# Expert stage: two up blocks moved ahead of two down blocks, gathers in blocks of three, results in halves

## What is computed

```python
H, E = 4, 24                       # four groups of 1024 tokens, 24 experts
C = math.ceil(2 * S / E)           # 86 places for each expert
def per_group(xf, lw, lb):         # xf: the group's 1024 tokens x 128
    combine, dispatch = top2_dispatch(xf, Wg, C)          # each token goes to two experts
    h = moe_apply(xf, combine, dispatch, W1, b1)          # 128 -> 512, both experts' rows added
    h = relu(layer_norm(h, lw, lb))
    return moe_apply(h, combine, dispatch, W2, b2)        # 512 -> 128
out = layer_norm(out + x, ln_out_w, ln_out_b)
x = x + layernorm(out)
```

## Time and profile before

| | before |
|---|---|
| median of 3 runs | 1206.05 us (1205.61 to 1211.87) |
| profiled execution, its own time | 1214.45 us |
| its span | 1212.7 us |
| PE busy in the span | 910.2 us (75%) |
| ACT busy | 793.9 us (65%) |
| DVE busy | 562.8 us (46%) |
| POOL busy | 378.3 us (31%) |
| mean granted clock of TensorE | 0.88 |

### The profile page before, as it was taken

One profiled execution on the slowest core, in us unless ns is written; L12 is line 12 of the kernel. 1 busy time (PEld: TensorE's weight loads), 2 busy tenths in 40 slices (PEclk: granted clock), 3 DMA queues, 4 the chain that ended last, 5 costly groups with the idle time before them and its releaser, 6 DMA issues. The chain is left out here.

```text
span 1212.7 us, 18733 instructions
## 1 busy us (share of the span) xinstructions
PE 910.2 (75%) x6570; PEld 431.7 (36%) x6570; DVE 562.8 (46%) x1894; ACT 793.9 (65%) x1181; POOL 378.3 (31%) x333
## 2 busy tenths in 40 slices
PE   4746974661599999999999999998499496594740
PEld 4633762330122222222222223323276364463640
DVE  7488767894001444344445153334351225326356
ACT  2133351453699999999999999994476483574720
POOL 6222442543300000000000000115572766866752
PEclk9657996886699999999999999998699698698875
DMA  3000005647921111111112121238786874966821
GB/s 98 1 1 1 1 1 129 162 114 203 324 78 49 52 46 61 52 61 52 61 52 62 53 61 30 64 79 238 163 167 198 136 175 127 169 173 142 154 68 50
DMA packets 83615, 118.37 MB, mean 98 GB/s; under 512 B 8974, under 2 KB 45583, under 8 KB 83410
## 3 DMA queue, kind: packets, MB, share of 16 engines
q1 hardware_dynamic: 67344, 88.72, 24.2%
q0 software_dynamic: 14752, 27.81, 13.6%
q10 hardware_dynamic: 1442, 0.86, 0.3%
HBM read 72.66 MB, written 44.70 MB: 97 GB/s over the span
## 5 line engine op out<-in xcount | busy, mean ns | idle before, releaser
L1466 ACT ACTIVATE s_e<-s_ps 128x1024 f32<-128x1024 f32 x512 | 486.9, 1025 | 30.0 <-PE s_ps L1615 29.4
L1628 PE MATMUL s_acc<-s_e,s_v 128*32 128x512 f32 x2048 | 274.5, 608 | 0.1
L1615 PE MATMUL s_ps<-s_q,s_k 64*128 64x512 bf16 x1024 | 196.0, 389 | 50.2 <-ACT s_e L1466 22.6
L1100 POOL DMA_INDIRECT x_in<-x_tokens,rows_of x72 | 70.2, 976 | 502.2 <-DVE rows_of L1259 456.0
L1615 PEld LDWEIGHTS s_ps<-s_q,s_k 64*128 64x128 bf16 x1024 | 49.2, 93 | 320.7 <-ACT s_e L1466 274.8
L1100 POOL DMA_INDIRECT e_hs<-h_rows,rows_of x72 | 116.3, 1615 | 65.0 <-DMA h_rows<-e_hs 42.0
L1888 PE MATMUL e_pn<-ident,e_hs 128*128 128x128 f32 x288 | 54.1, 307 | 78.4 <-DVE e_hs L2018 57.3
L1904 PE MATMUL e_py<-w,e_ht 128*96 128x128 f32 x768 | 103.0, 282 | 0.0
L1978 ACT ACTIVATE e_ht<-e_pn,ln_hid 128x288 f32<-128x288 f32 x192 | 84.8, 507 | 26.7 <-PE e_pn L1888 26.7
L1904 PEld LDWEIGHTS e_py<-w,e_ht 128*96 128x96 f32 x768 | 92.5, 170 | 0.0
L1962 ACT ACTIVATE l_so<-e_hs 128x512 f32<-128x512 f32 x72 | 45.2, 628 | 65.1 <-DMA e_hs<-h_rows,rows_of 62.4
(11 more groups left out here) (413 smaller groups left out, 1334.9 us busy)
## 6 DMA issues: line engine op xcount, KB each, us to landing
h_rows<-e_hs SPq DMA_DIRECT2D x72, 256.0 KB, 3.1
s_k<-stack_k SPq DMA_DIRECT2D x32, 512.0 KB, 4.5
s_q<-stack_q SPq DMA_DIRECT2D x32, 256.0 KB, 3.2
w<-in_w SPq DMA_DIRECT2D x1, 6144.0 KB, 21.7
y_rows<-e_ys SPq DMA_DIRECT2D x24, 192.0 KB
stack_q<-b_parts SPq DMA_DIRECT2D x8, 384.0 KB, 4.5
stack_k<-b_parts SPq DMA_DIRECT2D x6, 384.0 KB, 4.3
x_res<-in_x SPq DMA_DIRECT2D x4, 512.0 KB, 7.3
```

Source lines behind the costliest of these rows:

```text
L1100: nc.gpsimd.indirect_dma_start(dst, None, rows, bass.IndirectOffsetOnAxis(ap=idx, axis=0), compute_op=op).then_inc(R["landed"][k % FLIGHT] ...
L1466: nc.scalar.activation(E[g % 4][:, 2 * pair:2 * pair + 2, :], pS[pair][:].rearrange("p (a s) -> p a s", a=2), ACT.Exp, scale=SCALE).then_i ...
L1615: last = nc.tensor.matmul(pS[pair][:, a * CH:(a + 1) * CH], K[c % 2][rows, pair, j * P:(j + 1) * P], Q[c % 2][rows, pair, :], start=True, ...
L1628: last = nc.tensor.matmul(acc[hu % 2][32 * h:32 * h + 32, :], V4[c % 2][:, j, h, :], E[g % 4][:, h, :], start=j == 0, stop=j == TB - 1)
```

## The change

The change does five things. PE's fifth step of a group does the last two up blocks first, with the transposes of the last down block among them, and then the last two down blocks; since chunks of two blocks are then alive, there are six buffers of transposed chunks in place of four (`NHT`; the sixth is the tile `l_o`, free by then). The first x_transposes of the next group move from the end of the last up block to the place behind the first h_transposes of a group. POOL's gathers are ordered by blocks of three. The results of a group are gathered, normalised and stored in two halves. And DVE does these halves at other places: both halves of group 0 among group 2's results, group 1's and the first half of group 2's among the last group's.

```diff
-STAGES = (("x", 0, 0), ("x", 0, 1), ("x", 1, 0), ("h", 0, 0), ("x", 1, 1), ("x", 2, 0), ("h", 1, 0), ("x", 2, 1), ("y", 0, 0),
-          ("x", 3, 0), ("h", 2, 0), ("x", 3, 1), ("y", 1, 0), ("h", 3, 0), ("y", 2, 0), ("y", 3, 0))
+STAGES = ("x0 x1 x2 x3 x4 x5 x6 x7 x8 x9 "
+          "h0 h1 h2 h3 x10 h4 x11 h5 x12 x13 x14 x15 "
+          "h6 h7 h8 h9 x16 h10 x17 h11 x18 x19 y0 x20 x21 "
+          "h12 h13 h14 h15 x22 h16 x23 h17 y1 y2 "
+          "h18 h19 h20 h21 h22 h23 y3 y4 y5 y6 y7").split()
...
@@ PE
-            def up(n):
-                if n + 1 < NU:
+            def up(n, then=()):
+                if n % NB < NB - 1:
                     x_transposes(n + 1)
...
+                    for k in then[j:j + 1]:
+                        h_transposes(k // FC, k % FC)
...
+                    if h + 1 < GR:
+                        x_transposes(m + NB)
+                if j == NB - 2 and h + 1 < GR:
+                    h_transposes(m + 1, 0)
+                    h_transposes(m + 1, 1)
+                    up(m + NB, (FC * (m + 1) + 2, FC * (m + 1) + 3))
+                    up(m + NB + 1)
                 for c in range(FC):
                     down(m, c)
-                    if m % NB < NB - 1:
+                    if j < NB - 2 or j == NB - 2 and h + 1 == GR:
                         h_transposes(m + 1, c)
-                for n in beside(m):
-                    up(n)
+                if j < NB - 2 and h + 1 < GR:
+                    up(m + NB)
@@ ACT
-                for j in range(NB):
-                    if j < 3:
-                        std(m + j + (2, 2, 3)[j])
-                    if j < NB - 1:
-                        relu(m + j + 1)
-                    if j == 1:
-                        std(m + 4)
+                for j in range(NB - 2):
+                    if j < 2:
+                        std(m + j + 2)
+                    relu(m + j + 1)
+                    if 1 <= j <= 2:
+                        std(m + j + 3)
                     for n in beside(m + j):
                         hidden(n)
+                relu(m + NB - 1, range(0, 2))
+                for n in beside(m + NB - 2):
+                    hidden(n)
+                relu(m + NB - 1, range(2, FC))
@@ DVE
+                if h == 3:
+                    output(1, 0)
                 for j in range(2, NB):
                     result(m + j)
-                    if j == 3 and h < GR - 1:
-                        output(h - 1)
-            output(GR - 2)
-            output(GR - 1)
+                    if h == 2 and j in (2, 4):
+                        output(0, j // 2 - 1)
+                    if h == 3 and j in (2, 4):
+                        output(j // 2, 2 - j // 2)
+            output(2, 1)
+            output(3, 0)
+            output(3, 1)
```

166 lines of the change are left out of this document (94 added, 72 removed).

## The result

The changed kernel takes 1229.28 us in the median of 4 runs (1227.11 to 1233.36), the kernel before 1208.96 us in the 4 runs beside them (1205.61 to 1213.43). The ratio is 1.017, with a 95% interval of 1.0121 to 1.0219: slower by 15 to 26 us. The forecast was 1214.5 us and a range of 1207 to 1221. The direction was right, and the size was not.

A forecast was written before the change was run, and what follows sets the result against it. The prediction took POOL's partner gathers, then PE's up and down products, to bound the expert stage; 0 - 10.5 - 3.2 + 1.0 + 21.1 = +8.4 us on 1206.05 gave 1214.5 us, range 1207 to 1221.

The forecast's parts named there:

- The outputs: DVE from last scaling to end: six half outputs, small chains not shorter, 81.0 us against 59.9, so +21.1 us.
- Rival 3: Outputs: half an output costs half, and the gathers hide; +3.3 in place of +21.1, so 1196.7 us, faster; 4%.
- rival 5: Last group's result gathers starve beside DVE: those of (3, 0) end 13.4 us behind output(2, 1), total 1237 us; 2%.
- Boundary of groups 1 and 2: PE there: 12.1 us less from the moved down block and the vanished token wait, +1.6 for squares; sum -10.5 us.
- I take 1.6 of the 2.6 (ACT had about 1 us of slack there): Boundary of groups 1 and 2: the sixth block's squares on ACT, now right ahead of PSUM copies, cost PE +1.6 us.
- I cost this at nothing: POOL's gathers by blocks of three: two token blocks ahead of the last hidden block's six gathers, 7.5 us later, cost 0.
- Rival 4: Late rows: fifth and sixth block's rows come too late behind the tokens, 3 us at each boundary, +9, 1223.5 us; 10%.
- Boundary of groups 2 and 3: No token wait here: down block -3.8, squares +1.6, earlier first down block -1.0; sum -3.2 us.
- I take 0: Boundary of groups 0 and 1: the backlog of loads into `v_all` sets when the last hidden store lands; 0, ends -3 and +2.
- the token transposes are moved to where nothing waits for them: Boundary of groups 1 and 2, PE: the last up block, without token transposes, takes 3.2 us; no cost in their new place.
- The last group up to the last scaling: ACT's `std(23)` behind `relu(21)` makes scaled rows 2.0 us later, 1.0 given back without output stores among gathers; +1.0 us.
- the prediction's own sign of being wrong upward: If the three boundaries together give under 10 us, the kernel is slower than the range.

The follow-up runs named there:

- the second profile of before: The kernel before, unchanged, profiled once more: 1212.22 us.
- the slower set: Second of three sets of experiments: every kernel, the kernel before too (1284.96 us), took 6% longer than in the other two; only ratios within it are used.
- the third: Third set of experiments: there the kernel with outputs and squares back and loads later took 1196.15 us, ratio 0.989 to the kernel before.

## Why the prediction was right, and where not

**The outputs: right, and in size.** The mechanism (group 1's output moves out of a place where DVE waited, and the small chain doesn't shrink with the tiles) and its price, 21 us, are shown three times: 81.0 in the changed kernel, 81.1 in the kernel before with this alone, and 22 us less with it undone. Halves were forecast at 14.1 and 10.3 us and measure 14.4 and 10.5. That the sum is 81.0 to the tenth is partly luck: the six halves took 1.3 us more than forecast (78.3), the four results 0.4 less and the wait for gathers 0.8 less. Rival 3 (half an output costs half) is refuted, and so is rival 5, gathers that starve. From 1142 us on POOL issued 33 result gathers beside a DVE with hardly a gap:

```profile
L1105 POOL DMA_INDIRECT e_ya<-y_rows,take x33 | 32.0, 971 | 37.6 <-DMA y_rows<-e_ys 26.7 <-issue 9.1 <-DVE v_all L2093 1.7
```

A gather takes 971 ns there. The Trainium skill, "SBUF — State Buffer", has its "DVE blocks DMA" trap for the time in which DVE runs a 2-port perf-mode operation, and rival 5 took it for all of DVE's work. So the 971 ns speak against the rival; how far the rule itself holds is not shown, since no run here sorts DVE's instructions by mode.

**Boundary of groups 1 and 2: the mechanism right, 2.3 us too much.** The tokens' wait is gone; its part was forecast at 8.3 us, and with the halved gathers alone the interval is 9.5 us shorter. The last stretch, forecast at 8.2 us, took PE 8.95 (1004.99 to 1013.94). With the gathers in one row the boundary gives 11.3 us, more than the 10.5 forecast; the late rows took 3.2 of it back.

**"I take 1.6 of the 2.6 (ACT had about 1 us of slack there)": about right in size, one group short.** The squares cost 1.9 us of PE's waiting in each of three groups, and by the table above 1.4 net in group 1 at full clock. What the term left out is group 0, 2.1 us, where they delay the loads.

**"I cost this at nothing" for the gathers by blocks of three: this is the step that failed most.** Rival 4 (late rows, 3 us at each boundary, given 10%) is what happened at two of the three: the kernel with the gathers in one row is 3.2 and 3.0 us shorter there. The forecast set 7 us of margin against the time at which PE needs a row. But ACT needs it first, and ACT does squares ahead of the copies (the fifth block's in both kernels, the sixth's in the new order only), so a late row holds up PE's up block long before its own down block is due. The margin was measured at the wrong reader. In group 2 the two parts meet, and they had been costed apart. And the longer wait cost more than itself, since the clock behind it was 0.66 and not 1.00: of 3.1 us up to group 1's last up block, 1.2 are the wait and 1.7 the slower down block.

**Boundary of groups 2 and 3: +1.5 for -3.2.** Of the 4.7 us, 3.0 are the late rows. The first down block came 19.4 us behind P2 (20.5 before), as forecast. With the gathers in one row P3 comes 5.4 us behind the last up block, 4.2 before, and those 1.2 us are open.

**"I take 0" for the boundary of groups 0 and 1: right in mechanism, wrong at the end.** The backlog of the loads sets P1, 16.2 to 16.5 us behind their first issue in seven traces. The forecast said they start as before, "or up to 2 us longer, by the squares above", and took none of it. They started 3.0 us later, counted from P0. The squares are about 2 of it: with them in the old place the interval is 83.4 and not 85.2. Another 0.6 is the forecast's "the token transposes are moved to where nothing waits for them": they stand right ahead of the group's first down block, which comes 19.1 to 19.6 us behind P0 in every kernel of the table that has them there, and 18.5 to 18.9 in the others.

```profile
874.37 0.85 PE L1881 MATMUL e_px<-ident,x_in 128*128 128x128 f32 x3
875.01 0.64 PE L1922 MATMUL e_py<-bias_split,expert_hot 128*96 128x128 bf16 x4
```

**The last group up to the last scaling: +1.5 for +1.0.** Against the second profile of before it is +3.5, so this term's size is not settled. I had not seen one thing there. In the changed kernel `output(0, 1)` stands behind `result(16)`, whose down block now ends after the ups. It runs from 1096.99 to 1112.3, and the group's first scaling follows at 1113.0. In the kernel before with the outputs alone moved, the same output ends at 1099.9, and P3 to the last scaling is 40.2 us and not 44.6. Before the change a whole output stood there, and the first scaling came as late, 16.0 us behind P3 in both; what the change could have gained there it did not.

**The sum.** From P0 on the forecast was 9.2 us short: 7.0 at the second and third boundary (late rows and squares), 2.9 at the first (the loads), 0.5 in the last group, and 1.0 came back at the end of the span. That is the prediction's own sign of being wrong upward: the boundaries gave 3.9 us, under 10. In the medians the miss is 14.8 us (1229.28 for 1214.5). Of this 2.9 is the base: the forecast stood on the 1206.05 of three runs, and with the fourth the median is 1208.96. The difference between +17.6 from P0 and +20.3 in the medians is inside the interval (14.6 to 26.5).

**What is not settled.** When the clock falls behind a wait of 1.9 us and when it stays; why P3 comes later behind the last up block in one kernel than in another; and what the stretches in the slower set are (below).

## What to carry to other kernels

Cost a moved load or gather at its first reader, not at the engine that the stage is named after; and where two parts of a change lengthen the same chain (here an instruction moved ahead of a copy, and the data it waits for moved back), price them together. If the engine that waits is TensorE, look at the granted clock behind the wait as well. Small instructions in a dependent chain cost the same for half the data, so halve a tile only where the first half unlocks something that is waited for; and work in an engine's idle time is free only as long as it stays in it. Before a part is judged, undo the others: here the reordering of PE was worth 6 to 8 us and sat in a change that was 20 us slower, and with outputs and squares as before, nearly all partner gathers in one row and the loads later the kernel is at 0.989 of the time before.

## What the runs showed of the hardware

TensorE's granted clock behind a wait decides part of what the wait costs. In group 1 it was 0.66 over the five us behind a wait of 3.1 us and 1.00 behind one of 1.9 (gathers in one row), and a down block took 6.8 us and 5.1. But behind a wait of 1.9 us in the kernel with the squares back it was 0.66 too, so the length of that one wait does not settle it.

In the second set the same instructions stood still for times that no other set shows. In the kernel with outputs and squares back, ACT's copy behind an up block that PE had finished at about 1005 us came at 1028.63:

```profile
1010.28 0.48 ACT L1960 COPY e_xt<-e_px 128x384 f32<-128x384 f32 x1 [1.21 <-remote]
1028.63 0.69 ACT L1970 ACTIVATE e_hs<-e_ph,gate_of 128x512 f32<-128x512 f32 x1 [17.87 <-remote]
```

"remote" means that no instruction of this core is seen to have ended the wait. POOL issued its gathers at the usual 1.25 us all through it. There were such stretches in all four kernels of the set, in groups 1 and 2 above all: from P1 to P3 the kernel with the loads later took 198.1 us in this set and 154.2 in the third. Their cause stays open. By the ratio to the kernel before of its own set, this kernel is at 0.9812 in one and 0.989 in the other, and the two intervals don't meet.
